# A decoder stack on one core: the row loop written out, and a new order of work inside each step

## What is computed

```python
def attn_layer(x, Wqkv, qs, ksc, Wo):
    qkv = x @ Wqkv                       # 16 heads of 64
    q = l2norm(q) * qs; k = l2norm(k) * ksc
    q, k = rotary(q), rotary(k)
    out = local_attention(q, k, v)       # windows of 32, own and previous, softmax
    return out @ Wo
def ffn_layer(x, g, bln, W1, b1, W2, b2):
    xn = (x - mu) / sqrt(var + 1e-05) * g + bln
    a, gate = split(xn @ W1 + b1)        # 341 each
    return a * gelu(gate) @ W2 + b2
for i in range(6):
    x = attn_layer(shift_tokens(x), ...) + x
    x = ffn_layer(shift_tokens(x), ...) + x
```

## Time and profile before

| | us |
|---|---|
| median of three runs | 2140.3 (2137.77 to 2140.72) |
| the profiled execution | 2146.11 |
| its span | 2144.3 |
| TensorE busy | 1781.7 (83%) |
| VectorE busy | 1603.8 (75%) |
| GpSimd busy | 1354.0 (63%) |
| ScalarE busy | 1233.0 (58%) |
| chain that ended last: TensorE 46%, VectorE 18%, issue 12%, ScalarE 8% | |

### The profile page before, as it was taken

The page is one execution under the profiler, slowest core; times in us unless marked ns, Lnnn a source line. Parts: engine busy times, 40 slices in busy tenths (PEclk is TensorE's granted clock), DMA queues, the critical chain, the costliest instruction groups (busy, mean ns, idle before and its releaser), DMA issues.

```text
span 2144.3 us, 82361 instructions
## 1 busy us (share of the span) xinstructions
PE 1781.7 (83%) x32739; PEld 1426.5 (67%) x32739; DVE 1603.8 (75%) x4082; ACT 1233.0 (58%) x2424; POOL 1354.0 (63%) x1002
## 2 busy tenths in 40 slices
PE   2578858899888888888888888898888888889974
PEld 1444536777777777777777777776777767777763
DVE  2567768888788778777887887787788868878841
ACT  2345635566565566566655656665665666666641
POOL 2254536667677676667676666776677676767741
PEclk9789978999999999999999999999999999999985
DMA  4332341111211112111112112112112131121101
GB/s 160 115 136 108 142 150 39 37 30 35 90 32 47 42 37 69 54 45 37 46 35 86 29 45 51 37 51 72 38 31 57 27 96 29 45 51 37 30 17 44
DMA packets 83081, 126.44 MB, mean 59 GB/s; under 512 B 41866, under 2 KB 55490, under 8 KB 82498
## 3 DMA queue, kind: packets, MB, share of 16 engines
q1 hardware_dynamic: 77352, 119.58, 18.6%
q10 hardware_dynamic: 5402, 1.71, 0.3%
HBM read 42.63 MB, written 25.16 MB: 32 GB/s over the span
## 4 chain that ended last, share of the span: by engine, by line
PE 46%; DVE 18%; issue 12%; ACT 8%; POOL 2%; DVEq 1%; ACTq 0%; DMA 0%; SPq 0%; POOLq 0%
PE bank L1010 6%; PE bank L953 6%; PE bank L1022 6%; DVE qk_s L1423 5%; PE bank L1039 5%; PE bank L974 4%; PE bank L1041 3%; PE bank L1040 3%; DVE ssq L1435 3%; PE bank L933 3%; DVE qk_c L1412 3%; PE bank L987 3%; PE bank L925 2%; ACT f_h L1174 2%; DVE bank L1379 1%
## 5 line engine op out<-in xcount | busy, mean ns | idle before, releaser
L1244 POOL TENSOR_TENSOR qk_c<-qk_c,nrm 128x1024 f32<-128x1024 f32 x192 | 362.6, 1905 | 450.3 <-DVE nrm L131 450.3
L1292 POOL TENSOR_TENSOR qk_c<-qk_c,qk_s 128x1024 f32<-128x1024 f32 x192 | 452.0, 2375 | 24.6 <-DVE qk_s L1423 24.6
L1412 DVE TENSOR_TENSOR qk_c<-bank,rot 128x512 f32<-128x512 f32 x384 | 263.2, 685 | 183.6 <-ACT sq L1152 161.9
L1039 PE MATMUL bank<-w_hi,xT 128*128 128x512 f32 x576 | 278.4, 483 | 84.5 <-DVE qk_s L1423 77.4
L1152 ACT ACTIVATE sq<-bank 128x512 f32<-128x512 f32 x384 | 224.4, 606 | 207.6 <-PE bank L1041 193.5
L1423 DVE TENSOR_TENSOR qk_s<-bank,rot 128x512 f32<-128x512 f32 x384 | 260.9, 679 | 0.0
L1435 DVE TENSOR_REDUCE ssq<-sq 128x8 f32<-128x512 f32 x384 | 258.9, 674 | 0.0
L953 PE MATMUL bank<-ident,qk_c 128*128 128x128 f32 x1536 | 211.4, 283 | 54.8 <-issue 54.8
L1287 POOL TENSOR_TENSOR prob<-prob,pinv 128x512 f32<-128x512 f32 x192 | 196.9, 1049 | 76.8 <-DVE pinv L1401 76.8
L974 PEld LDWEIGHTS bank<-kT,qT 64*32 64x32 f32 x12288 | 188.9, 109 | 84.5 <-issue 84.1
L974 PE MATMUL bank<-kT,qT 64*32 64x64 f32 x12288 | 224.1, 222 | 12.1 <-issue 11.2
(11 more groups left out here) (150 smaller groups left out, 3621.1 us busy)
## 6 DMA issues: line engine op xcount, KB each, us to landing
v_back<-v_own SPq DMA_DIRECT2D x96, 384.0 KB, 3.9
front_raw<-in_L_ffn_Wqkv_dram SPq DMA_DIRECT2D x18, 512.0 KB, 5.5
w_high<-front_high SPq DMA_DIRECT2D x18, 512.0 KB, 2.7
w_low<-front_low SPq DMA_DIRECT2D x18, 512.0 KB, 3.6
w_hi<-w_high SPq DMA_DIRECT2D x18, 512.0 KB, 3.9
w_lo<-w_low SPq DMA_DIRECT2D x18, 512.0 KB, 4.7
v_back<-v_own SPq DMA_DIRECT2D x72, 128.0 KB, 2.4
wo<-in_L_ffn_Wo_dram SPq DMA_DIRECT2D x6, 512.0 KB, 6.3
```

The costliest lines, as they stand in the source:

```text
L1039: pe.matmul(bank[n % 2][:, :], xT[:, 1, lo:lo + P], w_hi[:, col:col + 512], start=True, stop=False)
L1244: pool.tensor_tensor(x, x, bcast(nrm[:, q.par(-1), HEADS * kind:HEADS * (kind + 1)], 2, DH), ALU.mult).then_inc(s["qkn"], 1)
L1292: pool.tensor_tensor(x, x, qk_s[:, kind, :], ALU.add).then_inc(s["rotd"], 1)
L1412: dve.tensor_tensor(qk_c[:, q.par(0), kind, 512 * half:512 * half + 512].rearrange("p (h d) -> p h d", d=DH), bank[n % 2][:, :].rearrange( ...
```

## The change

Three things.

1. The loop is gone: `rounds` writes out all 27 rows on every engine, so that every wait is for a constant.
2. Each engine's list within a step is in another order. TensorE: T1, TX, S0, S1, P2, P3, output projection, transposed probabilities, place 0, P4, place 1, P5, T0 of the next step, P0 of the next, A, P1 of the next, place 2. VectorE: cos, sin and square sum 0 and 1 first, then the norm chain threaded through mask, max and subtraction of the scores, and only then parts 2 and 3, then the sums of probabilities. GpSimd: `rotate` 0 goes ahead of `normalise`, `rotate` 1 stays behind it. ScalarE follows.
3. The FFN jobs are spread: 0 and 1 in step 2, 2, 3 and 4 (the gates) in step 3, 5 and 6 (values) in step 0 and 7 in step 1 of the row after.

```diff
-FFN_PLACES = {(2, 2): 0, (2, 4): 1, (2, 5): 2, (3, 1): 3, (3, 2): 4, (3, 3): 5, (3, 6): 6, (3, 5): 7}
+FFN_PLACES = {(2, 0): (0, 2), (2, 2): (1, 2), (3, 0): (2, 2), (3, 1): (3, 2), (3, 2): (4, 2),
+              (0, 0): (5, 3), (0, 2): (6, 3), (1, 0): (7, 3)}
+GATES, VALUES = {2: 0, 3: 1, 4: 2}, {1: 0, 5: 1, 6: 2}
     def rounds(eng, body):
-        for it in range(FIRST_LOOP):
-            body(it)
-        with eng.Fori(FIRST_LOOP, NIT - 1) as it:
-            body(it)
-        for it in (NIT - 1, NIT, NIT + 1):
+        for it in range(NIT + 3):
             body(it)
...
# SyncE: the FFN weights of a layer, before at row 2, step 0, after add_ffn of the row before
+                            if layer > 0 and row == 2 and j == 2:
+                                sp.wait_ge(s["f_p"], FJOBS * BATCH * layer)
+                                load_ffn(layer)
...
# ScalarE, copy_x
+                if q.j == 2:
+                    need(act, s["fadd"], q.it - 2)
...
# GpSimd, in body
                     low_x(q)
+                    if j == 1:
+                        ffn_product(it - 3, 2)
+                    if q.on(0):
+                        rotate(q, 0)
                     if q.on(-1):
                         normalise(q, 0)
-                    if j == 3:
-                        ffn_product(q, 0)
-                    if q.on(-1):
                         normalise(q, 1)
                     normalise_ffn(q)
                     if j == 2:
                         low_ffn(q)
...
                     if q.on(0):
-                        rotate(q, 0)
                         rotate(q, 1)
...
                     if q.on(-2):
                         normalise_prob(q, 0)
                         normalise_prob(q, 1)
+                    if j == 3:
+                        ffn_product(it - 2, 0)
+                    if j == 0:
+                        ffn_product(it - 3, 1)
...
# VectorE, in body, the new list of a step
+                        for n in range(2):
                             cos_part(q, n)
                             sin_part(q, n)
                             square_sum(q, n)
+                    norm_step(q, 0)
                     if q.on(-2):
                         k0 = score_mask(q, 0)
+                    norm_step(q, 1)
+                    if q.on(-2):
                         k1 = score_mask(q, 1)
...
+                    norm_step(q, 8)
+                    norm_step(q, 9)
+                    if q.on(0):
+                        cos_part(q, 2)
+                    norm_step(q, 10)
+                    if q.on(0):
+                        sin_part(q, 2)
+                        square_sum(q, 2)
                     if q.on(-4):
                         add_attention(q)
+                    if q.on(0):
+                        cos_part(q, 3)
+                        sin_part(q, 3)
+                        square_sum(q, 3)
```

More of the change, by code:

```diff
@@ L914, in ffn_job @@
                 if n == 0:
-                    pe.wait_ge(s["wf_in"], weights_due(q.it, 2, DMAS_FFN))
+                    pe.wait_ge(s["wf_in"], weights_due(row, 0, DMAS_FFN))
                     pe.wait_ge(s["f3"], row + 1)
@@ L937, in ffn_place @@
             def ffn_place(q, place):
-                if (q.j, place) in FFN_PLACES:
-                    ffn_job(q, FFN_PLACES[q.j, place])
+                n, back = FFN_PLACES.get((q.j, place), (None, 0))
+                if n is not None and round_on(q.it, back):
+                    ffn_job(q.it - back, n)
             def transpose_qk(q, kind):
@@ L1044, in body @@
             def body(it):
[L1045 to L1051, removed]
                 for j in range(GPB):
                     q = Step(it, j)
-                    ffn_place(q, 0)
                     if q.on(-2):
@@ L1056, in body @@
                         transpose_qk(q, 1)
+                    transpose_x(q)
+                    if q.on(-2):
+                        scores(q, 0)
+                        scores(q, 1)
+                    if q.on(0):
+                        project(q, 2)
+                        project(q, 3)
+                    if q.on(-4):
+                        out_proj(q)
+                    if q.on(-3):
+                        transpose_prob(q, 0)
+                        transpose_prob(q, 1)
+                    ffn_place(q, 0)
@@ L1210, in body @@
                     if q.on(-2):
-                        exponentials(q, 0)
+                        exponentials(q, 1)
+                    ffn_place(q, 0)
+                    if q.on(0):
+                        store_values(q, 0)
+                    ffn_place(q, 1)
                     if q.on(0):
                         store_values(q, 1)
-                    if q.on(-2):
-                        exponentials(q, 1)
+                    copy_x(q)
                     if q.on(-1):
@@ L1218, in body @@
                         store_qkT(q.next(), 1)
-                    copy_x(q)
+                    if q.on(1):
+                        squares(q.next(), 0)
                     if q.on(-3):
@@ L1222, in body @@
                         store_attT(q, 1)
[L1223 removed]
                     if q.on(1):
[L1225 removed]
                         squares(q.next(), 1)
[L1227 removed]
+                    ffn_place(q, 2)
             act.wait_ge(s["zeroed"], 5)
@@ L1496, in body @@
                     ffn_statistics(q)
+                    if j == 1 and round_on(it, 3):
+                        add_ffn(it - 3)
                 if links[0]:
```

116 lines of the change are left out of this document (37 added, 79 removed).

## The result

The changed kernel takes 2216.8 us, the median of four runs (2213.2 to 2228.8), against 2140.5 for the kernel before on the same chip: a ratio of 1.037, with a 95% interval of 1.033 to 1.041. It is slower by 76 us; the forecast was slower by 64. The profiled execution is the slowest of the four, 2228.8 us with a span of 2227.0, so the trace shows some 12 us more than the median.

A forecast was written before the change was run, and what follows sets the result against it. Rings of waits through several engines bound the kernel, none being full. Rows of 73.3 us plus 3.6 for late instructions give 76.9 against 74.1; with the ends +64: median 2204 us, 8-in-10 range 2112 to 2255.

The forecast's parts named there:

- The sum against the span: Whole span: rows 3 to 22 +56, rows 0 to 2 +8, row 23 +8, drain -8, together +64 us.
- the drain: End of the kernel: output projection now ahead of five FFN jobs, so 8 us less (0 to 15).
- The stops: TensorE pauses for late instructions in written-out bursts: 0.6 us an attend, 0.4 for scores, 3.6 us a row net.
- Ring A: VectorE and TensorE, mask 1 through sin 3, P5, attend, P1, cos 1 to next mask 1: 16.8 us without FFN.
- Ring B: Norm chain's end through GpSimd to `low_x`, TX, scores, mask 1 and back to the last norm step: 16.1 us.
- GpSimd's extras: Further GpSimd work per step: a product in steps 0 and 3, `low_ffn` in 2 (1.24 each), `normalise_ffn` in 1 (3.09).
- The place-0 jobs: FFN jobs on TensorE needing bank 7, held until `add_attention` has read it; a W1 job of 0.8 us costs 0.4.
- Step 1's price of 2.3 us: FFN job 7 on TensorE in step 1, 24 matmuls or 2.7 us, costs 2.3 us.
- job 3's table load: Job 3 at place 1 of step 3 waits for job 2's Gelu behind a ScalarE table load: 1.4 us.
- the 73.3 summed: A row from the longer ring of each step, 17.8, 19.2, 17.5 and 18.8 us, before late instructions are counted.
- the first rival: Instructions arrive in time in straight code: rows of 73.3 us, total 2120 us; chance 0.26.
- TensorE as the bound: Rival: the order packs tightly, TensorE's 64.6 us a row is the bound, 1950 us; chance 0.04.

The follow-up runs named there:

- the first experiment: The kernel before with only its row loop written out on every engine, order and FFN places kept: 2089.8 us, ratio 0.975.
- the kernel with both edits: The changed kernel with `add_attention` moved up on VectorE behind `score_sub` of the second half, and TX behind the scores on TensorE: 2133.9 us, ratio 0.996.
- after: The changed kernel itself, against the kernel before: 2216.8 us, ratio 1.037.
- the exchange of P1: The changed kernel with the next step's P1 ahead of the attend and its square ahead of the attend's copies: 2262.8 us; with TX behind the scores too, 2252.5 us.

## Why the prediction was right, and where it was off

**The rows.** 76.9 us forecast, 77.3 measured. Row 1 takes 71.5 (forecast 71.0), row 2 78.2 (76.1). The start and the end can't be measured by the norm step, since the new order puts it some 7 us later in a step. By P0, which stands at the end of the step before in both kernels, row 0 is 1 us longer ("a little") and begins 3 us later, and row 23 up to its P5 is 11 us longer (8 forecast); from there to the end it is 7 us shorter (8 forecast). The sum against the span is +82.7, forecast +64; rows 3 to 22 make 9 of the 19 us between, rows 1 and 2 some 3, and the rest lies ahead of row 0 and in row 23 and the drain. The profiled run is itself 12 us above the median, so the median came out closer.

**Writing out pays.** I took it from the looped rows against row 23 and from the jumps; shown by the first experiment, -51 to -56 us. The stops in attends cost there what I had read from rows 0 to 2: 33 us of attends in 20 rows, 0.41 a step against 0.6. (Rows 0 to 2 have nine attends and not eight; the 0.6 was summed over sixteen and stands.) The jumps were read from two rows: they cost 2.9 us on average and up to 5.3.

**Ring A, 16.8 us.** Its waits are there in step 2 of the kernel with both edits, shown above. Its lengths, read in the step of 16.63 us that is left when TX is late: mask 1 to the end of sin 3 7.58 (7.57 summed), from there to cos 1 6.27 (6.64), and to the next mask 1 2.59 (2.60), so 16.4. In 71 of the 80 steps of after, mask 0 waits over 0.3 us for the scores, for which the sum has no term. No run moved this ring alone.

**Ring B, 16.1 us plus GpSimd's extras.** Step 1, forecast at 19.2, takes 19.23 to 19.25 in the 8 of 20 rows without a stop or a slow clock in it. With `add_attention` ahead of the norm chain's end it takes 19.5 at the least, and only then does moving TX pay in full. That rings A and B are nearly equal was in the forecast; that a third runs from `add_attention` through place 0, attend and scores was not, and it made two of my later expectations fall (the exchange of P1, alone and with TX).

**The place-0 jobs.** That they wait for `add_attention` was forecast and is shown: 88 waits, 180 us. What the wait costs was forecast from the path alone. Step 1's price of 2.3 us holds: without ring B it takes 18.78, that is 16.4 and 2.3. Step 3 takes 18.3 and not 18.8, so job 3's table load costs less than 1.4. Steps 0 and 2 take 18.9 and 18.5 us by their medians and not 17.8 and 17.5. The term that was put at nothing is the clock: behind the 2 us wait it often falls, and P4, P5 and T0 run slow. Two executions of step 2 in after, neither with a stop in it, both with a wait of 2.2 us at place 0, by stretch:

```profile
1951.42:1969.77 18.35, 16.05 (x324) 13.77 (x323) 14.02 (x35) 11.52 (x23) 12.67 (x9) 0.91 0.12 31
1794.90:1812.23 17.33, 15.02 (x337) 12.53 (x327) 14.10 (x35) 11.51 (x23) 12.42 (x9) 1.00 0.28 87
```

At a mean granted clock of 0.91 the step takes 18.4 to 18.7 us, at 1.00 it takes 17.2 to 17.7, the forecast's 17.5. In rows 3 to 22 the clock falls 43 times, 147 us in all: 14 times in step 0, 8 in step 1, 13 in step 2 and 8 in step 3. Steps 1 and 3 are 1.2 us longer with it (20.4 against 19.2, 19.5 against 18.3). 43 x 1.1 = 47 us, or 2.4 a row. 38 of the 75 waits over 1.5 us at place 0 are followed by a fall; 4 of the other 5 falls come after a stop. With the wait at place 0 gone, step 0 has a median of 18.2, but the clock still falls for 119 us in all, now often behind TX's waits of 3 us; with TX late too it is 51.

**The stops.** Forecast 3.6 us a row, 2.4 of it in attends. Measured 2.1 a row, nearly all in scores. The cause that I had read, instructions coming late in blocks, is what the runs show: the numbers are those of blocks of 256, and every stop ends shortly after an instruction packet has landed. The size was wrong in both parts: 0.6 for an attend was read off rows in another order, where an attend is followed by other small work, and here it is some 0.03. For scores 0.4 was taken and about 0.5 found. A row without stops takes 75.2 us, 1.9 more than the 73.3 summed: 2.4 from the clock, less 0.5 in step 3. The stops came out 1.5 below the forecast. The two errors nearly cancel, and that 76.9 came so near is in part luck.

The Trainium skill ("Runtime: NRT & Kernel Launch", Instruction fetch mechanics), by which the fetch stays hidden in straight code, would make a row 77.3 - 2.1 = 75.2, so still slower than before: even with the stops gone the first rival would have fallen. By the stops at every written-out order here, the trace doesn't agree with the page.

**The rivals.** TensorE as the bound fell, as the waits of the profile after show. The written-out order of before with spread jobs, at 2069 us, is the nearest that any order here came to it.

## What to carry to other kernels

Before moving work, write down each ring that goes once round a step, with every engine in it, and compare their lengths: an edit that shortens one of two equal rings gives nothing, and says nothing about the other edit. Here 0 and 14 us alone became 83 together, and the wait that vanished at one place reappeared at another, by name, in the list of waits. Test the parts of a change alone: of these three, writing out the loop gave 2.5% and spreading the jobs another 1%, at 2069 us; the new order, with its own places for the jobs, took away 7% of that.

A shared bank is a place in the order, not a detail: a job put behind the output projection was held by an addition that nobody was in a hurry for.

## What the runs showed of the hardware

- In straight code TensorE stopped in every order tried, always at a number of its own instructions that is 0 or 255 modulo 256, mostly when that number falls near the end of a burst of small matmuls. The stops over 0.6 us last up to 3.8 us, 1.8 on average in after. Moving the count by 128 moves them; a projection inside the burst shortens them from 1.7 to 1.1 us; a second burst next to the first nearly doubles their number (23 to 40). Every stop ends 1.1 to 1.7 us after a packet of 16384 bytes has landed from the instruction queue.
- A jump back cost TensorE 1.7 to 5.3 us in one order, 2.9 on average, and 1.9 to 6.9 in another, 3.9 on average, with the same amount of work in the loop. Each of these waits ended 1.6 to 2.0 us after an instruction packet had landed.
- Behind about half of the waits of 2 us, once a step, the granted clock fell to its lower level, 1.2 GHz (147 us of rows 3 to 22; before, 58 us), and a step so hit was 1.1 us longer. A wait that seems covered can have this price too.
